# Splitting the expert matrices: from phase one, through DRAM, to the start of phase two; constant rows in eight pieces

## What is computed

```python
x = x + gnn(layernorm(x), adj, adj, Wq, Wk, Wv, Wo)
h = layernorm(x)
p = softmax(maximum(h @ gate_W + gate_b, 1e-4))
w = maximum(p, 0.1);  w = w / (sum of w over the top 2)
comb = w where the expert is in the top 2, else 0
x = x + einsum('bsef,bse->bsf', einsum('bsd,edf->bsef', h, expert_W) + expert_b, comb) / 2
```

## Time and profile before

| | us |
|---|---|
| median of 3 runs | 1747.8 |
| lowest and highest of them | 1744.1, 1752.78 |
| the profiled execution, its own time | 1740.44 |
| its span in the profile | 1738.5 |
| busy: TensorE, its weight loads | 1609.7 (93%), 1381.1 |
| busy: DVE, ACT, POOL | 1251.7, 981.0, 989.4 |
| DMA: bytes moved, mean rate | 385.40 MB, 222 GB/s |

### The profile page before, as it was taken

How to read it: one execution, slowest core, us unless ns; L and a number is a source line. 1 busy time by engine, 2 the same in 40 slices (tenths; PEclk the granted TensorE clock), 3 DMA queues, 4 the chain that set the end, 5 groups by cost and what they waited for, 6 DMA issues and landing times. The chain is left out here.

```text
span 1738.5 us, 43513 instructions
## 1 busy us (share of the span) xinstructions
PE 1609.7 (93%) x11856; PEld 1381.1 (79%) x11856; DVE 1251.7 (72%) x4692; ACT 981.0 (56%) x3117; POOL 989.4 (57%) x1723
## 2 busy tenths in 40 slices
PE   5899999999999999999999999997188999999996
PEld 4888888788888888888888888875066788888885
DVE  4668878788888888888888888886534555555554
ACT  3687777678777787777777778775111111111111
POOL 2345556556666666666665666656324465666554
PEclk9999999999999999999999999997599999999998
DMA  7777988878888888988888788783599988898886
GB/s 232 195 222 221 266 239 248 258 229 252 251 244 249 240 254 248 243 238 249 251 240 244 239 241 251 235 249 110 202 273 265 229 170 161 159 176 164 157 163 109
DMA packets 206364, 385.40 MB, mean 222 GB/s; under 512 B 22320, under 2 KB 31664, under 8 KB 206000
## 3 DMA queue, kind: packets, MB, share of 16 engines
q1 hardware_dynamic: 154144, 273.10, 54.8%
q0 software_dynamic: 29680, 69.55, 20.6%
q10 hardware_dynamic: 22304, 39.98, 7.1%
HBM read 206.26 MB, written 176.30 MB: 220 GB/s over the span
## 5 line engine op out<-in xcount | busy, mean ns | idle before, releaser
L622 ACT ACTIVATE prob<-prob,nmax 128x128 f32<-128x128 f32 x1024 | 398.7, 393 | 180.6 <-DVE amax L767 178.3
L1019 POOL TENSOR_TENSOR prob<-prob,rinv 128x512 f32<-128x512 f32 x256 | 261.9, 1044 | 205.2 <-DVE rinv L784 204.8
L1232 POOL DMA_INDIRECT out<-yt,token x135 | 211.8, 1569 | 213.5 <-DMA out<-yt,token 80.0
L763 DVE CUSTOM_DVE_ANT_0 prob<-ps_s,bias 128x128 f32<-128x128 f32 x1024 | 237.3, 287 | 104.8 <-PE ps_s L487 73.0
L1168 ACT ACTIVATE xgT_hi<-ps_x 128x512 fp32r<-128x512 f32 x135 | 80.8, 598 | 407.6 <-PE ps_x L1140 314.3
L1152 PE MATMUL ps_y<-we_hi,xgT_hi 128*128 x540 | 227.0, 420 | 19.4 <-DVE xgT_lo L1187 10.7
L1153 PE MATMUL ps_y<-we_lo,xgT_hi 128*128 x540 | 214.6, 397 | 0.0
L1154 PE MATMUL ps_y<-we_hi,xgT_lo 128*128 x540 | 214.4, 397 | 0.0
L660 ACT ACTIVATE pT<-ps_t 128x512 f32<-128x512 f32 x256 | 150.3, 587 | 79.7 <-PE ps_t L496 79.6
L622 ACT ACTIVATION_READ_ACCUMULATOR prob<-prob,nmax 128x1 f32 x1024 | 195.3, 191 | 0.0
L767 DVE TENSOR_REDUCE amax<-prob 128x4 f32<-128x512 f32 x256 | 175.7, 686 | 8.9
(11 more groups left out here) (151 smaller groups left out, 4334.1 us busy)
## 6 DMA issues: line engine op xcount, KB each, us to landing
ks<-kq_parts SPq DMA_DIRECT2D x192, 256.0 KB, 4.9
qs<-kq_parts SPq DMA_DIRECT2D x192, 256.0 KB, 6.2
xg<-x_lists ACTq DMA_DIRECT2D x135, 260.5 KB, 3.8
xin<-x SPq DMA_DIRECT2D x64, 256.0 KB, 8.0
kq_parts<-kT_hi SPq DMA_DIRECT2D x32, 512.0 KB
kq_parts<-kT_lo SPq DMA_DIRECT2D x32, 512.0 KB
kq_parts<-qT_hi SPq DMA_DIRECT2D x32, 512.0 KB
kq_parts<-qT_lo SPq DMA_DIRECT2D x32, 512.0 KB
```

Of the source, the lines that this page charges most:

```text
L622: last = nc.scalar.activation(prob[:, r, c, h, :], prob[:, r, c, h, :], ACT.Exp, bias=nmax[:, r, i:i + 1], scale=-1.0, accum_out=rsum[:, r ...
L763: last = nc.vector.tensor_tensor_reduce(out=prob[:, r, c, h, :], in0=ps_s[c % 2][:, P * h:P * h + P], in1=bias[:, b % 4, :], scale=-1.0, s ...
L1019: tt(prob[:, r, q], prob[:, r, q], rinv[:, r, HC * q:HC * q + HC].unsqueeze(2).to_broadcast([P, HC, P]), ALU.mult)\
L1232: pool.indirect_dma_start(out=out, out_offset=bass.IndirectOffsetOnAxis(ap=token[:, m, :], axis=0), in_=yt[:, r, :], in_offset=None, compu ...
```

## The change

The 32 preparation steps of phase one are gone, with `e_stage`, `e_hi`, `e_lo` and `e_parts`. In phase two SP loads the eight raw matrices into `we_lo`, all at once, then `e_bias`. ACT makes the eight high parts after it has issued the loads of tiles 0 to 4 and before the high part of tile 0; DVE makes the low parts in place, before the low part of tile 0. The constant rows are written in eight pieces, in the turns 7, 11, ..., 35: 128 spare rows and their ends in seven of them, and 128 rows of `out` in each.

```diff
 # phase one, SP
                     if ok(t - 2):
                         residual_in(t - 2)
-                    p = (t - 6) // 2
-                    if okp(p):
-                        hold(e_lo_done, p + 1)
-                        for i, part in enumerate((e_hi, e_lo)):
-                            sp.dma_start(e_parts[i, p], part[:, :].bitcast(f32)).then_inc(e_out, 16)
-                    p = (t - 4) // 2
-                    if okp(p):
-                        sp.dma_start(e_stage[:, :], v["expert_W"].rearrange("e d f -> (e d) f")[P * p:P * p + P, :]).then_inc(e_in, 16)
                     if ok(t - 1):
                         residual_in(t - 1)
...
-            sp.wait_ge(e_out, 32 * E * DC)
 # phase one, ACT
-            def rows_for_nobody(part):
-                spare = x_lists[E * LIST:ROWS, :].rearrange("(n p) d -> p n d", p=P)
-                if part == 0:
+            def rows_for_nobody(i):
+                if i == 0:
                     act.wait_ge(zeroed, 2)
                     act.wait_ge(consts_done, 6)
-                    act.dma_start(spare[:, :, 0:D], zero_tile[:, 0:D].unsqueeze(1).to_broadcast([P, E - 1, D])).then_inc(spare_out, 16)
-                    act.dma_start(spare[:, :, D:W], spare_end[:, :, :]).then_inc(spare_out, 16)
-                else:
-                    act.dma_start(out[T:T + DUMMY, :].rearrange("(n p) d -> p n d", p=P), zero_tile[:, 0:D].unsqueeze(1).to_broadcast([P, E, D])).then_inc(spare_out, 16)
+                if i < E - 1:
+                    at = E * LIST + P * i
+                    act.dma_start(x_lists[at:at + P, 0:D], zero_tile[:, 0:D]).then_inc(spare_out, 16)
+                    act.dma_start(x_lists[at:at + P, D:W], spare_end[:, i, :]).then_inc(spare_out, 16)
+                act.dma_start(out[T + P * i:T + P * i + P, :], zero_tile[:, 0:D]).then_inc(spare_out, 16)
...
-                    p = (t - 4) // 2
-                    if c == 3 and t % 2 and okp(p):
-                        act.wait_ge(e_in, 16 * p + 16)
-                        if p >= 1:
-                            act.wait_ge(e_out, 32 * p)
-                        nc.scalar.activation(e_hi[:, :], e_stage[:, :], ACT.Copy).then_inc(e_hi_done, 1)
...
-                    if c == 1 and t in (9, 15):
-                        rows_for_nobody(0 if t == 9 else 1)
+                    if c == 1 and t % 4 == 3 and 0 <= (t - 7) // 4 < E:
+                        rows_for_nobody((t - 7) // 4)
 # phase one, POOL
-                    p = (t - 4) // 2
-                    if c == 3 and odd and okp(p):
-                        hold(e_hi_done, p + 1)
-                        tt(e_lo[:, :], e_stage[:, :], e_hi[:, :].bitcast(f32), ALU.subtract).then_inc(e_lo_done, 1)
 # phase two, SP
             for e in range(E):
-                for i, w in enumerate((we_hi, we_lo)):
-                    sp.dma_start(w[:, e * DC * D:(e + 1) * DC * D].bitcast(f32).rearrange("p (c f) -> p c f", c=DC),
-                                 e_parts[i, DC * e:DC * e + DC].rearrange("c p f -> p c f")).then_inc(parts_in[e], 16)
-                    if e or i:
-                        sp.wait_ge(parts_in[e], 16 * i + 16)
-                sp.sem_inc(experts_in, 1)
-                if e == 0:
-                    sp.dma_start(e_bias[:, :], v["expert_b"].rearrange("(a e) f -> a (e f)", a=1).to_broadcast([P, E * D])).then_inc(ebias_in, 16)
+                sp.dma_start(we_lo[:, own(e)].bitcast(f32).rearrange("p (c f) -> p c f", c=DC),
+                             v["expert_W"][e].rearrange("(c p) f -> p c f", p=P)).then_inc(raw_in[e], 16)
+            sp.dma_start(e_bias[:, :], v["expert_b"].rearrange("(a e) f -> a (e f)", a=1).to_broadcast([P, E * D])).then_inc(ebias_in, 16)
 # phase two, ACT
                 for j in range(N):
+                    if g == -1 and j == N - 1:
+                        for e in range(E):
+                            act.wait_ge(raw_in[e], 16)
+                            nc.scalar.activation(we_hi[:, own(e)], we_lo[:, own(e)].bitcast(f32), ACT.Copy).then_inc(we_hi_done, 1)
                     t = tile(g, j + 1)
 # phase two, DVE
+            for e in range(E):
+                dve.wait_ge(we_hi_done, e + 1)
+                tt(we_lo[:, own(e)], we_lo[:, own(e)].bitcast(f32), we_hi[:, own(e)].bitcast(f32), ALU.subtract).then_inc(experts_in, 1)
```

More of the change, by code:

```diff
@@ L84, in build @@
     kq_parts = nc.dram_tensor("kq_parts", [2, 4, 2, P, D], f32, kind="Internal").ap()
-    e_parts = nc.dram_tensor("e_parts", [2, E * DC, P, D], f32, kind="Internal").ap()
     top = ExitStack()
@@ L122, in phase_a @@
     const_in, ident_in, fill_done = v["const_in"], v["ident_in"], v["fill_done"]
-    x, adj, x_lists, e_parts, out = v["x"], v["adj"], v["x_lists"], v["e_parts"], v["out"]
+    x, adj, x_lists, out = v["x"], v["adj"], v["x_lists"], v["out"]
     kq_parts = v["kq_parts"]
@@ L176, in phase_a @@
         spare_end = sb("spare_end", [P, E - 1, 1 + E])
-        e_stage = sb("e_stage", [P, D])
-        e_hi = sb("e_hi", [P, D], f32r)
-        e_lo = sb("e_lo", [P, D], f32r)
         ps_s = [pb("ps_s0"), pb("ps_s1")]
@@ L199, in phase_a @@
         spare_out, padded, tab_step = sem("spare_out"), sem("padded"), sem("tab_step")
-        e_in, e_hi_done, e_lo_done, e_out = sem("e_in"), sem("e_hi_done"), sem("e_lo_done"), sem("e_out")
         bias_done = sem("bias_done")
@@ L400, in _ @@
             sp.wait_ge(fill_done, 1)
-            sp.wait_ge(spare_out, 48)
+            sp.wait_ge(spare_out, 16 * (3 * E - 2))
             for e in range(E):
@@ L1079, in phase_b @@
     const, ident, fill, ends, zero_tile, tab = v["const"], v["ident"], v["fill"], v["ends"], v["zero_tile"], v["tab"]
-    x_lists, e_parts, out = v["x_lists"], v["e_parts"], v["out"]
+    x_lists, out = v["x_lists"], v["out"]
     R = RING
@@ L1099, in phase_b @@
         ps_y = [v["pb"](mem, f"ps_y{i}", [P, 512], f32) for i in range(R)]
-        ebias_in, parts_in = sem("ebias_in"), sems("parts_in", E)
+        ebias_in, raw_in, we_hi_done = sem("ebias_in"), sems("raw_in", E), sem("we_hi_done")
         experts_in = sem("experts_in")
@@ L1109, in tile, with own @@
             return Item(g, N, off, TILES)
+        def own(e):
+            return slice(e * DC * D, (e + 1) * DC * D)
         def turns(body):
```

## The result

| | before | after |
|---|---|---|
| median of 4 runs | 1750.29 | 1725.18 |
| lowest and highest | 1744.1, 1757.32 | 1721.44, 1732.38 |
| the profiled execution, its own time | 1740.44 | 1723.66 |
| its span | 1738.5 | 1721.9 |
| first gate product to that of the 29th pair (28 pairs) | 1023.8 | 1006.7 |

All times are us. A few executions fall into a slower state, and all medians from here on leave these out. Phase one became 23.6 shorter and phase two 7.0 longer.

A forecast was written before the change was run, and what follows sets the result against it. The prediction took TensorE to bound both phases except at three disturbed places. Terms -10 - 3 - 5 + 3 = -15 us took the profiled execution from 1740.4 to 1725.4, the median from 1747.8 to 1733; range 1720 to 1750.

The forecast's parts named there:

- Constants, -10: Phase one: writing constant rows in eight pieces removes nearly all of two slow pairs' 11.5 us excess, less 1.5: -10 us.
- Expert preparation in the middle, -3: Middle of phase one: removing expert preparation gives mainly DMA relief, bounds 0 and 10 us, taken as -3.
- engine time freed gives nothing: Middle of phase one: TensorE is the bound, so freeing ACT, POOL and SP time there gains 0 us.
- Over 15 us would mean that DMA paced it: Sign of error: phase one's middle shorter by more than 15 us would mean DMA, not TensorE, paced it.
- Run-out, -5: End of phase one: without expert subtractions on POOL, delays of 6.4 us go; taken as -5, between 3 and 6.4.
- Phase two, +3: Phase two: first product 22 us later, mostly recovered because adds keep up without weights; +3 us, bounds -2 and +18.
- the two small terms (-1.4 and +1): Phase two's end: 1.4 us returns as transposes run a tile ahead; 1 us added for long single adds.
- Loads slow: Rival, phase two: loads at 270 GB/s and nothing recovered, phase two +30, total +12, 1760 us; chance 0.10.
- lag stays: Rival, phase two: loads fast but everything moves by 18.3 us, cancelling phase one's gain, 1748 us; chance 0.13.
- Pieces stall: Rival, phase one: eight constant-row pieces cost 1.5 to 2 us each, giving back the 10; 1743 to 1745; chance 0.08.

The follow-up runs named there:

- e1: Kernel before with only the constant rows changed, written in eight pieces; 1779.55 us, ratio 0.996 to before.
- e2: Changed kernel with the constant rows turned back to two bursts in turns 9 and 15; 1758.89 us, ratio 0.9841 to before.
- e0: The changed kernel itself, run again as reference; 1747.33 us, ratio 0.9788 to before.
- e9: Changed kernel with each expert split just ahead of its tile, half the bias loaded behind the second expert, half behind the eighth; 1709.72 us, ratio 0.979 to before.
- e3_again: Same kernel as e3, run again beside e8 on another chip; 1739.8 us.
- e8: Same as e3, but POOL's subtraction replaced by a memset that reads no SBUF; 1725.73 us.
- e3: Changed kernel with ACT's copy and POOL's subtraction put back in phase one on a tile of zeros, no DMA; 1779.52 us.
- e4: Changed kernel with the expert loads and stores (24 MB) put back in phase one, no engine work; 1752.4 us.
- e6: Changed kernel with each expert split just ahead of its tile and the whole bias loaded behind the second expert; 1741.04 us, ratio 0.9762 to before.
- e5: Changed kernel with each expert split just ahead of its tile, bias still loaded last; 1745.25 us, ratio 0.9781 to before.

## Why the prediction was right, and where its steps were off

The forecast was 1733 and "faster", from -15 us in the profiled execution; that came out at -16.8, and the median at 1725.18, inside the range. That the sum came so close is in part luck: phase one gained 5.6 us more than the forecast's 18, and phase two cost 4.0 more than its 3. The medians moved by 25, and the 8 beyond the profiles are no term of the prediction. The terms, from the two profiles and the runs:

- **Constants, -10: right for the two pairs, open for the pieces.** The two pairs gave 11.8 us. e1 gave 8 us (its interval is 3 to 11), e2 against e0 some 9 (ratios 0.9841 and 0.9788). In the first chip's profile the eight pairs with a piece took 36.8 us and the others 35.6, with a wait of 0.7 to 1.7 us before scores in seven of them; that would take 9.5 us back, and e9 shows none of it. The clock had its part in it: from 332 to 340 us, at and behind the second stall, the granted clock of before is 0.52 to 0.63. That was in the 42.73 already.
- **Expert preparation in the middle, -3: the wrong mechanism.** The step that failed is "engine time freed gives nothing". The other 26 pairs gave 5.3 us on the first chip, the products that wait for DVE came 8.5 us earlier there, e3_again against e8 shows 13 where the traffic is out of the way, and e3 against e4 27 on a chip with longer pairs. The prediction priced DVE's held operation, 1.7 us, once at the run-out and did not ask whether the 31 subtractions before it did the same. TensorE being busy 97.6% hid waits of some tenths of a microsecond in every pair, part of them inside its busy time.
- **"Over 15 us would mean that DMA paced it": fell.** The middle did get 17.1 shorter, but e4 carries all the DMA traffic and costs nothing visible.
- **Run-out, -5: right,** at 6.3, and so is its make-up: 1.6 us for the hold on DVE where the prediction had 1.7, and 4.1 for the rest where it had 4.7 before its discount (e3_again, e8 and e9). In the timeline after, `key`, the operation that took 1.85 us, takes 0.17 at 1208.8. The row does not put all of the 1.7 on the subtraction: DVE's operation began 0.54 us before it.
- **Phase two, +3: mis-sized,** at +7.0. Loads went nearly as worked out (387 to 392 GB/s), the last landing at 28.2 for 26.7, first product at +33.3 for 32.3: 1.0. Tile 0 took 4.9 us (1260.63 to 1265.52) and not 4.5, as nine of its twelve products and not seven ran before the granted clock rose from 0.5; TensorE had stood still for 22.8 us up to the first of them, where before two groups of transposes ran in the 3.2 us ahead: 0.4. DVE has tile 2's low part (1266.79), which waits for ACT's copy, ahead of tile 0's sum (1267.91), a wait that before lay under that for the bias: 2.3. Together 3.7. The last 0.4 is what the two small terms (-1.4 and +1) were to bring: no row priced them, and they came to about nothing. The five adds (28.2 for 28.25) and the copies of tiles 10 to 134 (400.8 for 401) came to the microsecond: without weights in the queues the adds keep up.
- **Rivals.** "Loads slow" and "lag stays" are out by the adds and the copies. "Pieces stall" wanted 1.5 to 2 us a piece and 1743 to 1745: the time is not that, and e1 and e9 have pairs with pieces as short as the others, but its sign, waits in the turns with pieces, was there in the first profile.

The prediction cites some 358 GB/s a core from the Trainium skill, "HBM Reference", section "Specifications (TRN2)"; it does not bind here, where the trace shows 387 to 392 over 20 us.

## What to carry to other kernels

When one small operation on VectorE shows several times its usual time, look at the minimum and median of all its instances: if the median is the long one, it is a term for every turn, and a GpSimd operation that reads SBUF beside it is the first suspect, even when that operation's result is due much later. A kernel at 97% TensorE can still lose 0.8% to waits of a few tenths of a microsecond that stand in each turn (e3_again against e8), and its idle time shows only part of them; compare the starts of the same products in two traces. When work moves to the head of a phase, count what stands behind it in order on each engine, not only when its loads land: three attempts at this start each fell short of their expectation, by a bias that landed later, by a third expert that landed later, and by splits that stood in order behind a tile.

## What the runs showed of the hardware that was not expected

- A TENSOR_TENSOR of 128x16 on DVE, 0.14 us alone, took 1.22 beside a two-input POOL operation of 1.28 and 0.14 beside a memset of 0.95. A TENSOR_SCALAR of 128x16 with one input took 0.75 us beside POOL's product and ended 0.03 us behind it, where it takes 0.2 otherwise; that it was held is read from these rows alone.
- The same program ran with different alignments of DVE and POOL on different chips, each held through the middle of its run: pairs of 36.0 us on average or of 36.7 (the changed kernel), of 36.2 or 37.7 (e3). So the change is worth 1.35% on one chip and 2.1% on another. For e3, 28 pairs are 41.9 us apart between its two chips and the times 39.7; before differs by 35 to 38 between the same kinds of chip. That this is its whole cause was not shown, since the profile of before is from the first chip alone, and whether the chip or something else sets the alignment is not known.
- The 2 MB bias is read from 16 KB for all partitions: with it ahead, ACT's copy of the third expert began 20.8 us into phase two (e6), with half of it ahead 18.6 (e9), with none 14.9 (e5, the same order on ACT) and 14.7 (the changed kernel).
